# Selective scan on one core: VectorE takes the second product in six units of a batch instead of four, and rows of B and C are stored at unit 22 of the running batch

## The reference

```python
x = einsum('ed,bld->bel', in_proj_w, hidden)
u = silu(causal_conv4(x) + conv_b)
dt_lo, Bm, Cm = split(einsum('ke,bel->bkl', x_proj_w, u))
delta = softplus(einsum('er,brl->bel', dt_proj_w, dt_lo) + dt_proj_b)
# per t: state = state * exp(delta * A) + (delta * u) * B_t ;  y_t = sum over n of state * C_t
y = (y + D * u) * silu(z)          # z is the layer-normed running x, which y is added to
```

## Time and profile before

| what | value |
|---|---|
| median of 3 runs | 4152.42 us (4151.8 to 4153.67) |
| the profiled execution | 4150.07 us, of it 4148.3 us span |
| PE, DVE busy over the span | 3649.8 us (88%), 2860.9 us (69%) |
| ACT, POOL busy over the span | 1818.7 us (44%), 1435.3 us (35%) |
| stage m0, units | from 96.08 to 571.24 us of the span |
| stage m3, units | from 3160.05 to 3611.62 us |

### The profile page before, as it was taken

The page is one execution under the profiler, slowest core; times in us unless marked ns, Lnnn a source line. Parts: engine busy times, 40 slices in busy tenths (PEclk is TensorE's granted clock), DMA queues, the critical chain, the costliest instruction groups (busy, mean ns, idle before and its releaser), DMA issues. The chain is left out here.

```text
span 4148.3 us, 47410 instructions
## 1 busy us (share of the span) xinstructions
PE 3649.8 (88%) x15419; PEld 1758.1 (42%) x15419; DVE 2860.9 (69%) x4137; ACT 1818.7 (44%) x3051; POOL 1435.3 (35%) x1030
## 2 busy tenths in 40 slices
PE   6999856999999999898999879785886999689898
PEld 2333323555555555542333344343333333244454
DVE  2888888578777884457888256627667899934663
ACT  4666542222222221243777443336665666321244
POOL 1999854122211220054000100003445999700122
PEclk8999987999999999997999989896998999899999
DMA  3555441122233212365775110001004555502420
GB/s 100 141 155 147 129 127 57 50 93 74 68 103 100 81 31 74 116 144 102 79 79 56 55 61 0 3 0 64 10 0 130 149 151 148 141 18 71 80 56 22
DMA packets 249833, 338.37 MB, mean 82 GB/s; under 512 B 45602, under 2 KB 147522, under 8 KB 248036
## 3 DMA queue, kind: packets, MB, share of 16 engines
q1 hardware_dynamic: 249620, 335.70, 32.5%
HBM read 284.38 MB, written 53.35 MB: 81 GB/s over the span
## 5 line engine op out<-in xcount | busy, mean ns | idle before, releaser
L757 ACT ACTIVATE m_dA<-m_delta,m_a_neg 128x512 f32<-128x512 f32 x512 | 347.2, 689 | 328.1 <-DVE m_H_bank L827 255.3
L1926 DVE TENSOR_REDUCE a_core_minus_max<-a_core_a 128x1 f32<-128x512 f32 x512 | 317.1, 684 | 57.2 <-PE a_core_a L1752 57.2
L570 PE MATMUL m_y<-m_H,ident 128*128 128x512 f32 x512 | 279.9, 634 | 80.9 <-DVE m_H L844 80.3
L777 POOL TENSOR_TENSOR m_dB<-m_du,m_BC 128x1024 f32<-128x1024 f32 x128 | 301.6, 2357 | 123.3 <-DVE m_du L807 84.7
L766 POOL TENSOR_TENSOR m_H<-m_H,m_BC 128x512 f32<-128x512 f32 x224 | 285.0, 1272 | 63.5 <-DVE m_H L836 60.6
L1878 ACT ACTIVATE X<-a_core_s 128x512 f32<-128x512 f32 x512 | 264.6, 603 | 92.7 <-PE a_core_s L1752 92.6
L777 POOL TENSOR_TENSOR XN<-m_du,m_BC 128x1024 f32<-128x1024 f32 x128 | 301.3, 2361 | 2.7 <-DMA m_BC<-bc_ready 2.7
L1318 POOL TENSOR_TENSOR ctxT<-ctxT,f_scales 128x1024 f32<-128x1024 f32 x48 | 103.7, 2159 | 531.7 <-DVE ctxT L1143 531.7
L578 PE MATMUL m_y<-m_H,ident 128*128 128x512 f32 x512 | 271.5, 619 | 2.5 <-POOL m_H L766 2.4
L1278 ACT ACTIVATE XN<-f_g,f_power_back 128x512 f32<-128x512 f32 x128 | 88.0, 687 | 404.1 <-PE f_g L1215 404.1
L1384 DVE SCALAR_TENSOR_TENSOR XN<-f_u,f_power_back,XN 128x512 f32<-128x512 f32 x128 | 95.8, 749 | 226.9 <-PE f_u L1215 226.9
(11 more groups left out here) (419 smaller groups left out, 8321.9 us busy)
## 6 DMA issues: line engine op xcount, KB each, us to landing
m_BC<-bc_rows SPq DMA_DIRECT2D x224, 512.0 KB, 4.9
XN<-in_L_ffn_w_dram SPq DMA_DIRECT2D x72, 256.0 KB, 2.7
m_BC<-bc_ready SPq DMA_DIRECT2D x32, 512.0 KB, 4.9
ternary<-ctxT SPq DMA_DIRECT2D x96, 128.0 KB, 1.7
a_core_q<-a_q_parts SPq DMA_DIRECT2D x48, 256.0 KB, 12.9
a_core_k<-a_k_parts SPq DMA_DIRECT2D x48, 256.0 KB, 14.6
f_w_tern<-ternary SPq DMA_DIRECT2D x24, 512.0 KB, 6.1
f_core_q<-f_q_parts SPq DMA_DIRECT2D x24, 512.0 KB, 8.1
```

Source lines behind the costliest of these rows:

```text
L570: pe.matmul(ps_y[:, 0, :], ident[:], HD[n % NH], start=False, stop=True, skip_group_check=True).then_inc(s_ad, 1)
L757: act.activation(dA[:, i % NA, :], delta[b % 2][:, e, :], ACT.Exp, scale=a_neg[:, e, k % N:k % N + 1]).then_inc(s_dA, 1)
L777: pool.tensor_tensor(dB[n % ND][:], du[b % 2][:, h * EH:(h + 1) * EH, :], BC[n % NS][:, 0:1, :].broadcast_to([P, EH, L]), ALU.mult).then_i ...
L1926: dve.tensor_reduce(mx[u % 2][:, qt, h:h + 1], ps_a[:, at % NR, 0:n], AX.X, ALU.max, negate=True).then_inc(s_red, 1)
```

## The change

`OWN` gains 9, so units 9 and 25 of every batch are own as well: 16 products go from POOL to DVE (2 units x 4 batches x 2 stages). SP stores the next batch's rows of B and C just ahead of unit 22's load instead of between the batches, and the eight weight transfers of batch 1 in stage m0 go behind the rows of its unit 8.

```diff
-        OWN = (5, 12)
+        OWN = (5, 9, 12)
...
-        LAG = 3
+        LAG, STORE = 3, 22
...
-            for b in range(NB):
+            def store_rows(b):
+                sp.wait_ge(s_dblc, b + 1)
+                sp.dma_start(bc_parked if b == B else bc_dram[b], xdbl[R:W, :]).then_inc(s_bcd, 16)
+
+            if not given:
+                store_rows(0)
+            for b in range(B):
                 if b >= FIRST:
-                    sp.wait_ge(s_dblc, b + 1)
-                    sp.dma_start(bc_parked if b == B else bc_dram[b], xdbl[R:W, :]).then_inc(s_bcd, 16)
                     sp.wait_ge(s_bcd, 16 * (b + 1 - FIRST))
-                if b == B:
...
-                    break
-                if then and b == 1:
-                    sp.wait_ge(s_wt, 1)
-                    nxt.load_small(sp)
-                    nxt.load_rows(sp)
                 for k in range(NS if b < FIRST else 0, NU):
+                    if k == STORE and b + 1 < NB:
+                        store_rows(b + 1)
                     rows_of(b, k)
+                    if then and (b, k) == (1, NU // 4):
+                        sp.wait_ge(s_wt, 1)
+                        nxt.load_small(sp)
+                        nxt.load_rows(sp)
+            if then:
...
+                sp.wait_ge(s_bcd, 16 * NB)
```

More of the change, by code:

```diff
@@ L441, in _ @@
                     park_or_load(i, 1)
-            for b in range(NB):
+            def store_rows(b):
[4 more added lines that the diff above has]
+            for b in range(B):
                 if b >= FIRST:
-                    sp.wait_ge(s_dblc, b + 1)
-                    sp.dma_start(bc_parked if b == B else bc_dram[b], xdbl[R:W, :]).then_inc(s_bcd, 16)
                     sp.wait_ge(s_bcd, 16 * (b + 1 - FIRST))
-                if b == B:
[L448 to L453, removed]
-                    break
-                if then and b == 1:
-                    sp.wait_ge(s_wt, 1)
-                    nxt.load_small(sp)
-                    nxt.load_rows(sp)
                 for k in range(NS if b < FIRST else 0, NU):
+                    if k == STORE and b + 1 < NB:
+                        store_rows(b + 1)
                     rows_of(b, k)
+                    if then and (b, k) == (1, NU // 4):
[3 more added lines that the diff above has]
+            if then:
+                sp.wait_ge(s_du, NB * EB)
+                sp.wait_ge(s_del, NB * EB)
+                for i in range(3):
+                    for h in range(2):
+                        park_or_load(i, h)
+                sp.wait_ge(s_park, 96)
+                sp.wait_ge(s_bcd, 16 * NB)
         def first_weights(pe):
```

## The result

| | before | after |
|---|---|---|
| median of 9 runs (us) | 4151.80 (4148.22 to 4155.39) | 4163.76 (4157.33 to 4166.83) |
| profiled execution (us) | 4150.07, span 4148.3 | 4165.53, span 4163.8 |
| both scan stages, units only (us) | 926.7 | 939.0 |

The ratio is 1.0026, with a 95% interval of 1.0017 to 1.0034: 7 to 14 us slower. The forecast was +6.7 us, in a range of -3 to +15 about the median then known.

The account below looks back on a forecast made before the run. VectorE was taken to bound the scan stages, with GpSimd in step behind it. Unit 25 +8.8, unit 9 +0.5 and the store -2.6 gave +6.7 us: 4159.1 us on the median 4152.42, own range 4156 to 4162, whole range 4149 to 4167.

Parts of the forecast that it names:

- VectorE sets the pace; GpSimd's time is worth nothing: Both scan stages: VectorE never rests in a batch's second half, GpSimd follows in step; sparing GpSimd 1.27 us a product buys nothing.
- Unit 25 costs 1.10 us a batch: Unit 25 as an own unit takes 4.53 us instead of 3.43, nothing hides it: +8.8 us over eight batches.
- A reading of mine: Stage m3's quiet batch: GpSimd's dB for unit 28, 3372.69 to about 3375.04, just meets VectorE's scan at 3375.05.
- Unit 9 is hidden: The hole between units 9 and 10, 2.41 us to spare, covers the own product's 1.10 us; seven batches pay nothing.
- the term of +0.5: Unit 9 in batch 3 of stage m3, whose hole has only 0.64 us to spare: about +0.5 us.
- The store gives 2.6: Boundary between batches 0 and 1 of stage m0 shrinks from 42.23 to about 39.6 us: -2.6 us.
- The clock: TensorE's half-clock hits on its convolution lengthen the hole behind unit 9 by 1.70 us each, in none to seven batches.
- Rival B: Half-clock hits in all seven convolving batches instead of three: +6.8, in all +13.5 us, 4165.9; chance 0.13.
- Rivals C and D: C: unit 9 paid in full, +14.4 in all, 0.08. D: moved weights leave first boundary unmended, +10.4, 0.07.
- within 0.2%: Whole kernel: median between 4144.1 and 4160.7 us, not told from no change; chance 0.60.

## Why the prediction was right, and where it was off

- *VectorE sets the pace; GpSimd's time is worth nothing.* Right, and shown: with GpSimd alone relieved (2.0 us a batch) the clean batch stayed at 113.49 us and the kernel within 5 us, not 20 faster.
- *Unit 25 costs 1.10 us a batch.* Right in every profile that has it, 8.7 us in all with the last batch's 1.03. Alone it measured +11.6 (6.6 to 16.2), which holds it. Moved to unit 23 it costs nothing in a batch with a hole there (5.45 us with and without).
- *A reading of mine was wrong.* I took GpSimd's dB at 3372.69 for unit 28's. Unit 28's starts at 3369.15; the buffers' names show it, since units 30 and 31 write to XN. The one of the earlier trace rows is unit 29's. So GpSimd did not just meet VectorE there but was some 3.5 us ahead. The conclusion stood for a better reason than I gave.
- *Unit 9 is hidden.* Right in the rows (5.53 us with and without), but the term of +0.5 was mis-sized: the changed kernel shows 0.4 in the batch without a full hole and 1.1 from the odd 0.36 us in three batches of stage m3, 1.5 in all (1.1 is left of the +4.5 above without the clock, since units 9 of two other batches came out 0.3 shorter). Alone unit 9 measured +5.0 (1.2 to 8.7), more than any row of it accounts for; what else is in that median is open.
- *The store gives 2.6.* Right alone (-2.62 in the stretch) and in the changed kernel (41.29 less one hit of 1.70 is 39.59, against 42.23). The single runs do not add up to it, since own unit 25 alone already fills 1.4 us of that hole; the forecast's sum is not touched by that.
- *The clock.* Rival B in part. The profile I started from had three slowed convolutions; the changed kernel's had five. Over the profiles of kernels that keep own unit 5 it was three to five of seven, with old own units as with new, so nothing shows it as the change's doing. It accounts for 3.4 us between the two profiled executions, just the two more hits from which the rival was said to decide, and for an unknown part between the medians.
- *Rivals C and D* fall: unit 9 was hidden, and the boundary lost its hole.
- *Sum.* The median of 4163.76 lies in the stated range of 4149 to 4167, but above the forecast's own 4156 to 4162, and +6.7 lies just below the interval of 7 to 14. The mechanism was right and the sum too small: the unit 9 term has 1.5 us in the rows instead of 0.5, and there was no term for the L257 product (+2.4) or for more hits of the clock (+3.4) in the profiled execution. The last two vary from execution to execution, so that their whole weight fell on one side there is chance. With the sum the call of "within 0.2%" failed, which had been given 0.60.

## What to carry to other kernels

Work moved between two engines that are both about 90% busy (here 857 and 820 us of 927) is not judged by their totals. It costs where it lands: here 1.1 us in a unit without a hole behind it, nothing two units earlier. Put it just ahead of a wait that something else ends. The other way round, taking work from a unit just ahead of such a wait (unit 21) buys nothing, since the wait grows by as much. Check with a run that only relieves the other engine whether that one's time is worth anything.

## What the runs showed of the hardware

An own unit seems to cost TensorE its clock. The 2.35 us that TensorE waits ahead of the convolutions come from own unit 5, which makes VectorE's next product late. With units 9, 12, 23 and 28 the same place reads (stage m0, batch 2):

```profile
341.69 1.13 PE L576 MATMUL m_y<-m_H,ident 128*128 128x512 f32 x2 [0.36 <-DVE m_H L850]
...
344.81 1.13 PE L576 MATMUL m_y<-m_H,ident 128*128 128x512 f32 x2 [0.70 <-DVE m_H L850]
345.77 3.60 PE L539 MATMUL m_w<-m_xin,m_taps 128*128 128x512 f32 x8
```

Two short waits instead of one long one. The convolution's matmuls over the whole kernel, ns min/median/max, in the changed kernel and then in this one:

```profile
L539 PE MATMUL m_w<-m_xin,m_taps x256: 590/592/1061, 40.4 to 3445.5; 128*128 128x512 f32 x128
```

```profile
L539 PE MATMUL m_w<-m_xin,m_taps x256: 590/592/593, 40.3 to 3419.6; 128*128 128x512 f32 x128
```

Not one ran at 1.2 GHz any more, nor in the two kernels with three own units (594 at most). In the eleven profiles with own unit 5 three to five batches of seven had such matmuls, and a full hit lengthens the hole behind unit 9 from 2.61 to 4.31 us, by 1.70. Each kernel has one profiled execution. Own unit 21 is gone from these kernels too, and that it is the length of the wait, and not something else that goes with unit 5, was not tried by itself.
